# Attention heads on one core: ScalarE takes the next head's exponentials before it rounds the probabilities that came back

## The reference

```
x1 = x + layernorm(attention(layernorm(x)))
   q, k, v = xn @ W_Q[h] + b_Q[h], ...            per head h
   scores  = q k^T / sqrt(128), causal mask
   attn    = softmax(scores)
   z       = attn v ;  out = sum over h of z W_O[h] + b_O
out = x1 + layernorm(mlp(layernorm(x1)))
   mlp(t) = (gelu(t Wg^T) * (t Wu^T)) Wd^T, hidden size 2048, weights unpacked from 4-bit words with a scale per 32
```

## Time and profile before

| | |
|---|---|
| median of three runs | 1606.38 us |
| profiled execution, own time | 1606.72 us |
| its span, first to last instruction | 1604.8 us |
| TensorE matmuls busy | 1577.9 us, 98% of the span |
| VectorE, ScalarE, GpSimd busy | 66%, 61%, 44% |
| mean granted TensorE clock | 0.998 |
| scores of the 128 heads | from 18.2 us to 1041 us of the span |

### The profile page before, as it was taken

How to read it: one execution, slowest core, us unless ns; L and a number is a source line. 1 busy time by engine, 2 the same in 40 slices (tenths; PEclk the granted TensorE clock), 3 DMA queues, 4 the chain that set the end, 5 groups by cost and what they waited for, 6 DMA issues and landing times.

```text
span 1604.8 us, 28430 instructions
## 1 busy us (share of the span) xinstructions
PE 1577.9 (98%) x9600; PEld 1398.1 (87%) x9600; DVE 1060.9 (66%) x3074; ACT 975.6 (61%) x2433; POOL 711.6 (44%) x1069
## 2 busy tenths in 40 slices
PE   6999999999999999999999999999999999999998
PEld 5888899889888988888889888888888888888887
DVE  4666677677767677677767766665656556565665
ACT  5887677767776777677767766644444444444443
POOL 5764455445554455455445533333333333333333
PEclk9999999999999999999999999999999999999999
DMA  4653434434443444443444455561000010000000
GB/s 122 186 172 116 129 128 149 142 116 142 149 139 119 142 142 137 127 151 126 142 128 136 142 157 162 155 214 40 27 14 27 14 40 27 14 28 14 27 15 25
DMA packets 157440, 167.69 MB, mean 104 GB/s; under 512 B 15856, under 2 KB 130672, under 8 KB 157296
## 3 DMA queue, kind: packets, MB, share of 16 engines
q1 hardware_dynamic: 157296, 165.89, 32.8%
HBM read 94.53 MB, written 71.30 MB: 103 GB/s over the span
## 4 chain that ended last, share of the span: by engine, by line
PE 85%; DMA 6%; ACT 3%; DVE 2%; SPq 2%; issue 1%; POOL 1%; DVEq 0%; POOLq 0%
PE fbank L692 14%; PE fbank L694 14%; PE fbank L693 14%; PE obank L694 7%; PE obank L693 7%; PE obank L692 7%; PE ubank L692 5%; PE ubank L693 5%; PE ubank L694 5%; PE ubank L716 3%; DMA turned_scratch<-turned 3%; PE fbank L794 3%; DMA back<-turned_scratch 2%; SPq L494 2%; ACT probs L589 1%
## 5 line engine op out<-in xcount | busy, mean ns | idle before, releaser
L692 PE MATMUL fbank<-xnT_hi,weights 128*128 128x512 f32 x768 | 305.8, 398 | 1.1 <-DVE xnT_lo L870 1.1
L693 PE MATMUL fbank<-xnT_lo,weights 128*128 128x512 f32 x768 | 304.7, 397 | 0.0
L694 PE MATMUL fbank<-xnT_hi,weights 128*128 128x512 f32 x768 | 304.6, 397 | 0.0
L1238 POOL TENSOR_TENSOR pT_lo<-back,pT_hi 128x512 fp32r<-128x512 f32 x128 | 165.9, 1296 | 284.9 <-ACT pT_hi L654 284.9
L600 ACT ACTIVATE w_raw<-fbank 128x512 f32<-128x512 f32 x128 | 76.4, 597 | 262.7 <-PE fbank L694 262.7
L1200 POOL TENSOR_SCALAR probs<-probs,rsum 128x128 f32<-128x128 f32 (+1 forms) x512 | 208.9, 427 | 20.6 <-DVE rsum L893 16.7
L694 PEld LDWEIGHTS fbank<-xnT_hi,weights 128*128 128x128 f32 x768 | 145.1, 189 | 35.2
L885 DVE CUSTOM_DVE_ANT_0 probs<-ubank,mask 128x128 f32<-128x128 f32 (+1 forms) x512 | 155.0, 355 | 29.1 <-PE ubank L694 28.3
L692 PEld LDWEIGHTS fbank<-xnT_hi,weights 128*128 128x128 f32 x768 | 145.2, 189 | 27.0 <-DVE xnT_lo L870 1.5
L693 PEld LDWEIGHTS fbank<-xnT_lo,weights 128*128 128x128 f32 x768 | 145.2, 189 | 24.7
L974 DVE SCALAR_TENSOR_TENSOR w_raw<-w_raw,fbank 128x512 f32<-128x512 f32 x128 | 87.9, 687 | 113.3 <-ACT w_raw L600 113.3
(11 more groups left out here) (122 smaller groups left out, 4571.9 us busy)
## 6 DMA issues: line engine op xcount, KB each, us to landing
turned_scratch<-turned SPq DMA_DIRECT2D x128, 384.0 KB, 2.6
back<-turned_scratch SPq DMA_DIRECT2D x512, 96.0 KB, 2.2
w_raw<-in_w_pairs SPq DMA_DIRECT2D x32, 256.0 KB, 3.3
w_hi_scratch<-w_hi SPq DMA_DIRECT2D x48, 128.0 KB, 2.0
w_lo_scratch<-w SPq DMA_DIRECT2D x48, 128.0 KB, 2.0
weights<-w_hi_scratch SPq DMA_DIRECT2D x24, 256.0 KB, 3.6
weights<-w_lo_scratch SPq DMA_DIRECT2D x24, 256.0 KB, 4.1
x_res<-in_x SPq DMA_DIRECT2D x16, 256.0 KB, 2.9
```

Source lines behind the costliest of these rows:

```text
L692: nc.tensor.matmul(out, a[0], b[0], start=start, stop=False, skip_group_check=skip)
L693: nc.tensor.matmul(out, a[0], b[1], start=False, stop=False, skip_group_check=skip)
L694: return nc.tensor.matmul(out, a[1], b[0], start=False, stop=stop, skip_group_check=skip)
L1238: pool.tensor_tensor(lo[:].rearrange("p u b (a j) -> p (u b) a j", j=32), mem.back[m % 2][:, :, 0:2].rearrange("p a u b j -> p (u b) a j") ...
```

## The change

ScalarE gets a list of its own, `scalar_steps`: in every step that has both, pT of head n-1 is taken out and put back right behind the scores (for ScalarE: the exponentials) of head n+1. That holds for steps 1 to 126. The lists of the other engines, the SyncE queue, every tile, every semaphore and every instruction stay as they are. Line numbers behind line 134 move up by 10.

```diff
+def scalar_steps():
+
+    for n in range(STEPS_ALL + 1):
+        plan = step_plan(n)
+        if ("scores", n + 1) in plan and ("pT", n - 1) in plan:
+            plan.remove(("pT", n - 1))
+            plan.insert(plan.index(("scores", n + 1)) + 1, ("pT", n - 1))
+        yield from ((n, kind, m) for kind, m in plan)
...
-    for n, kind, m in STEPS:
+    for n, kind, m in scalar_steps():
         c, j, h = n // HEADS, n % HEADS, m % HEADS
```

## The result

The changed kernel takes 1636.99 us (median of four runs, 1635.31 to 1639.13), the kernel before in the same comparison 1605.85 us. The ratio is 1.0193, 95% interval 1.0175 to 1.021: slower by 31 us, where 1638 was forecast. The profiled execution took 1635.31 us, 28.6 more than the one of before.

The account below looks back on a forecast made before the run. TensorE, hardly ever stopping, was taken as the bound. 31.4 us (24 piece periods) + 2.3 (7 other periods) - 2 (DMA waits) = +31.7 on 1606.72, so 1638.4; the runs' median is 0.3 lower: 1638 us, range 1612 to 1660.

Parts of the forecast that it names:

- The floor of 31.55 us per period: TensorE's gapless time for four steps: 4 x 6.51 us, plus 5.51 us for the values of one.
- the busy share as a sign: In the changed kernel's trace, TensorE's busy time was to stay and its share fall to 96%.
- Point 1: ScalarE's order pT, q, k: next scores at E + 4.88, under the free 5.05; no cost, 0.17 us spare.
- E: The start of a head's exponentials on ScalarE, from which the prediction counts its times in us.
- Point 2: TensorE's z waits for GpSimd's `pT_lo`: z at E + 3.87, scores at E + 5.02, just under 5.05.
- Point 3: GpSimd's `normalise` queues behind `pT_lo`: exponentials to exponentials 6.69 us against a step of 6.51, 0.18 us late.
- Point 4: Ring exponentials, pT, `pT_lo`, `normalise`, piece, `w_hi`, z, exponentials: E + 7.67, 1.16 us over a step, in 24 periods.
- Open by 2.4 us: The claimed room, before the change, in the loop from exponentials through `normalise` and the weight piece back to exponentials.
- The rule beside the row: GpSimd's `pT_lo` waits for one 0.39 us `spread` instruction in 24 periods: +9.4 us, 1648 us; chance 0.08.
- the piece stays hidden: Rival: `normalise` ends earlier, so only 0.33 us per period is lost: 1615 us; chance 0.14.
- the other 24 pieces pay too: Rival: the value matmuls' 5.51 us cover is used up, adding 28 us: 1666 us; chance 0.08.
- it is faster: Rival: exponentials no longer wait for DMA behind pT: about 1600 us, 1585 at best; chance 0.07.

Follow-up runs that it names:

- run 11: The kernel before, with the change applied only in steps n mod 4 = 0: 1605.91 us, ratio 1.0005 to the kernel before.
- run 12: The changed kernel, with the change undone in steps n mod 4 = 3 and n mod 16 = 2 (output evacuation): 1606.16 us, ratio 1.0005.
- run 1: The changed kernel, with the change undone in steps n mod 4 = 3 alone: 1609.72 us, ratio 1.0035 to the kernel before.
- run 5: The changed kernel, with ScalarE's rounding of the weight piece behind pT and GpSimd's lo part behind `pT_lo`, in steps n mod 4 = 0: 1638.15 us.
- run 4: The changed kernel, with VectorE's `spread` in steps n mod 4 = 3 moved between z's lo part and the inverted sums: 1636.49 us, ratio 1.0196.
- run 10: The kernel before, with the change applied to steps 1 to 16 alone: 1602.79 us, ratio 0.9997 to the kernel before.
- run 2: The changed kernel, with the change undone in steps n mod 4 = 0 alone: 1635.96 us, ratio 1.0191 to the kernel before.
- run 9: The changed kernel, with GpSimd's `pT_lo` of steps n mod 4 = 3 put behind the next step's `normalise`: 1633.19 us, ratio 1.0179.
- run 7: run 5 with the piece's lo part behind the next `normalise`, and `spread` (n mod 4 = 3) ahead of z's lo part: 1641.27 us.

## Why the prediction was right

**What bounds the kernel.** The floor of 31.55 us per period and the search for who makes a step longer held. What did not: the busy share as a sign. It was to fall to 96% and stayed at 98%, and the idle rows of TensorE for `pT_lo` were to hold 25 to 30 us, over a us at a time, and hold 15.3 us, 0.44 to 0.68 at a time but for the first (1.23); another 7.5 us are in the longer records of the same matmuls. Intervals between the same matmul of two steps show the loss whole: summed over the 128 heads, scores to scores, they grew by 29.2 us.

**Point 1**, ScalarE's own line at E + 4.88, had room in ordinary steps (TensorE's waits for k's lo part are mostly those that the held VectorE causes).

**Point 2**, z at E + 3.87 and "just under" the limit, was just over it: 0.08 us per moved step (run 11), not nothing. And with no room left on this way, it missed the step with the evacuation, where the exponentials are late by themselves and `pT_lo` with them: 7 x 0.77 = 5.4 us (7.42 against 6.65). This term was left out of the sum; run 12 shows it.

**Point 3**, the loop through `normalise`, 6.69 us, was too long by 0.1: steps 50 and 51 have their exponentials at 435.72 and 442.30, 6.58 us. The term that was off is `pT_lo` to `normalise`, 1.27 (444.77 to 446.04) and not 1.35.

**Point 4**, the ring through the piece, came out at 7.63 for 7.67, with every stage within 0.08 us. Undoing the change at its entry gives back about 25 of 31 us (run 1). But the lateness was taken for 1.31 us in one interval, and in the trace it is spread: 0.08, about 0.4 and 0.8. The middle part is the held `spread`, a second cause that the prediction does not have on this side. By itself it would make the exponentials 0.48 us late and not 1.12: run 5 opened the ring and the exponentials of that step still came 6.99 us after the ones before (441.89 to 448.88). The two lie side by side and overlap: taking away the smaller alone gains next to nothing (run 4), and the larger alone leaves the smaller to be paid (run 5). Only undoing the move opened both at no price.

One reading in point 4 is wrong. "Open by 2.4 us" is what the change adds on GpSimd (`normalise` from E + 1.38 to E + 3.81), not the room that there was: by the same rows the way before was 1.38 + 1.63 + 0.04 + 1.29 to `w_hi` and 1.57 from there to the exponentials (501.60 to 503.17), 5.91 us, or 0.6 us below a step. Nothing in the sum hangs on it.

**The sum.** It agrees with the measured time partly by luck. The profiled execution is 28.6 us longer, where 31.7 was summed up; its intervals grew by 29.2. The 24 piece periods were to cost 31.4 us and cost 26.5 in the two intervals at the piece (1.10 each, and not 1.31; in the period shown above it is 1.27), and the held VectorE is part of that. What the table calls the rest cost 2.1 us, for 2.3. The evacuation's 5.4 us were missing. The gain was taken as 2 us, from the waits for DMA; the value steps and transposes became 4.8 us shorter. That this is a gain of the change is not shown: run 10 has 2.9 us of it in chunks that it does not change. So the errors are -4.9, -0.2, +5.4 and -2.8 us, and the largest two cancel.

**The rule beside the row.** The chance of 0.08 for GpSimd being held was the right page and the wrong side. GpSimd's `pT_lo` has a mean of 1292 ns (1296 before), and its `normalise` beside the rest of `spread` takes 1.73 us in step 52 and not 1.63; VectorE was held, by 1.05 us. The Trainium skill (SBUF — State Buffer, section "SBUF: two separate sides") says that whichever starts first keeps the ports for its whole instruction, and here the trace agrees: `pT_lo` began 0.1 us ahead of L962. The 1648 us did not follow from that rule, as the prediction has it; it needed VectorE to start first, which the rule leaves open. I applied the rule only to the victim that lay on my path, and priced it by the short instruction and not by the long one.

**The rivals.** That the piece stays hidden is refuted by the exponentials that follow `w_hi` and z without a gap (449.03, 449.35, 449.93) and by the interval behind them, which falls from 7.31 to 6.75 when they no longer wait for the piece (run 5). That the other 24 pieces pay too did not happen (12.06 us in the value step, 6.59 behind it), though runs 2 and 5 show how little was missing. That it is faster: the DMA waits nearly vanished, but that they had cost TensorE anything is not shown. Run 10 keeps only that gain, in the first chunk, and cannot be told from no change.

## What to carry over

A wait on an idle engine is not free room if queues are in order: find what stands behind the moved instruction on every engine that it feeds, and follow that until it comes back to where it started. A ring longer than the step is a loss in each step, however idle every engine looks. When one experiment opens a ring and the time stays, compare the intervals, not the total: the loss may have changed places, or a second, smaller one was lying under it.

## What the runs showed of the hardware

A VectorE instruction of 0.23 us that starts just behind a GpSimd one of 1.29 us takes 1.28 us (444.87), and 1.33 us when it is another one of the same kind (run 9). All four `spread` instructions behind the first have been caught so in one of the traces (L969 of run 7 takes 1.37 us at 613.06). The GpSimd instruction keeps its length. Beside the shorter instructions of `normalise` the same one takes 0.39 us. VectorE instructions that read PSUM are not touched: `qT_lo` starts inside a `pT_lo` of GpSimd 70 times in the changed kernel and takes 0.48 us, as it does with GpSimd idle. Nor are its block transposes: in the kernel before, the two of a step (L1043) take 1.02 us with GpSimd at work beside them throughout (45.59) and 1.03 us with GpSimd idle (149.43). Which other VectorE instructions can be held was not tried one by one.

TensorE's record of a matmul that waits a little can be a longer matmul and no idle time: the first of z (L702) has a mean of 354 ns over its 256 in the changed kernel and had 325 ns before. The interval between the same matmul of two steps has no such gap.
